# Mask products in couples, and the last rows of two weight matrices stacked, in a two-layer attention and expert kernel

## What is computed

```python
x = L0_attn_x                                  # (8, 512, 256)
xn = layernorm(x)
# layer 0: causal attention, 16 heads of 64, rotary q and k, and a dense gated FFN of 768
sim = q @ k.T * scale
sim = where(causal, sim, -inf)
s = softmax(sim) @ v @ Wo + bo
g = silu((silu(xn @ wg.T) * (xn @ wu.T)) @ wd.T)
x = x + s * g
xn = layernorm(x)
# layer 1: attention without a mask, 16 heads of 16, and 8 experts; expert e takes 64 tokens of each batch
s = attention1(xn)
gate = einsum('becd,edf->becf', xe, w1)        # d = 256, f = 704
up   = einsum('becd,edf->becf', xe, w3)
out  = einsum('becf,efd->becd', silu(gate) * up, w2)
x = x + s * silu(out)
```

## Time and profile before

| what | value |
|---|---|
| median of 3 executions | 2100.8 us (2099.96 to 2102.17) |
| the profiled execution's own time | 2100.51 us |
| its span, first to last instruction | 2098.8 us |
| PE busy | 1930.3 us, 92% |
| DVE, ACT, POOL busy | 1442.2, 1288.3, 666.4 us |
| mean granted TensorE clock | 0.977 |

### The profile page before, as it was taken

How to read it: one execution, slowest core, us unless ns; L and a number is a source line. 1 busy time by engine, 2 the same in 40 slices (tenths; PEclk the granted TensorE clock), 3 DMA queues, 4 the chain that set the end, 5 groups by cost and what they waited for, 6 DMA issues and landing times. The chain is left out here.

```text
span 2098.8 us, 39214 instructions
## 1 busy us (share of the span) xinstructions
PE 1930.3 (92%) x12160; PEld 1474.2 (70%) x12160; DVE 1442.2 (69%) x2908; ACT 1288.3 (61%) x3069; POOL 666.4 (32%) x1032
## 2 busy tenths in 40 slices
PE   1999999999999999999999689994999999999997
PEld 1877878777878788788788578883556556656653
DVE  5785885876858858858678554422777777777773
ACT  3675674664656746646566565531686786776774
POOL 0353452543543534525435223332001011011012
PEclk9999999999999999999999889997899999999999
DMA  6110211111111111111111373312000011011001
GB/s 221 41 41 25 49 41 33 40 32 42 42 32 41 42 32 44 39 42 36 26 41 41 118 275 105 103 61 100 4 18 22 30 50 50 0 50 50 0 31 40
DMA packets 72942, 111.82 MB, mean 53 GB/s; under 512 B 5952, under 2 KB 46784, under 8 KB 72256
## 3 DMA queue, kind: packets, MB, share of 16 engines
q1 hardware_dynamic: 72224, 108.62, 17.5%
q10 hardware_dynamic: 544, 1.05, 0.2%
HBM read 55.12 MB, written 20.97 MB: 36 GB/s over the span
## 5 line engine op out<-in xcount | busy, mean ns | idle before, releaser
L1518 DVE TENSOR_REDUCE nm<-ps 128x1 f32<-128x512 f32 x512 | 336.8, 687 | 114.6 <-PE ps L1377 110.8
L1629 ACT ACTIVATE pt<-pst 128x512 f32<-128x512 f32 x512 | 296.0, 602 | 142.4 <-PE pst L1385 141.4
L805 POOL TENSOR_SCALAR pr<-pr,rinv 128x128 f32<-128x128 f32 (+3 forms) x512 | 264.8, 538 | 359.4 <-DVE rinv L691 359.4
L570 ACT ACTIVATE pr<-sc,nmax 128x128 f32<-128x128 f32 (+3 forms) x512 | 266.2, 528 | 141.3 <-DVE nmax L680 139.8
L811 POOL TENSOR_TENSOR qk<-ra,rb 128x256 f32<-128x256 f32 x256 | 183.9, 740 | 243.5 <-DVE rb L702 187.6
L680 DVE TENSOR_REDUCE nmax<-sc 128x1 f32<-128x128 f32 (+3 forms) x512 | 219.9, 483 | 57.8 <-PE sc L405 57.6
L1377 PE MATMUL ps<-kb,qb 96*128 96x512 f32 x512 | 238.2, 467 | 12.6 <-DVE nm L1518 10.0
L1385 PE MATMUL pst<-qb,kb 128*128 128x512 f32 x512 | 208.1, 408 | 6.7 <-ACT pt L1629 3.6
L403 PE MATMUL sc<-k,qs 128*128 128x256 f32 (+2 forms) x512 | 205.4, 403 | 1.3 <-DMA k<-k 1.2
L1377 PEld LDWEIGHTS ps<-kb,qb 96*128 96x128 f32 x512 | 97.7, 191 | 144.2 <-DVE nm L1518 95.6
L417 PE MATMUL w<-ident,pr 128*128 128x128 f32 x1280 | 172.1, 282 | 22.7 <-DVE rb L702 18.1
(11 more groups left out here) (203 smaller groups left out, 4703.5 us busy)
## 6 DMA issues: line engine op xcount, KB each, us to landing
k<-k SPq DMA_DIRECT2D x256, 128.0 KB, 2.2
raw<-in_w SPq DMA_DIRECT2D x16, 704.0 KB, 5.5
raw<-in_w SPq DMA_DIRECT2D x8, 640.0 KB, 5.1
xa<-in_x SPq DMA_DIRECT2D x2, 2048.0 KB, 13.8
x<-in_x SPq DMA_DIRECT2D x8, 512.0 KB, 3.6
x_scratch<-x SPq DMA_DIRECT2D x8, 512.0 KB, 3.4
xt_hi_scratch<-xt_hi SPq DMA_DIRECT2D x1, 4096.0 KB, 13.6
xt_lo_scratch<-xt_lo SPq DMA_DIRECT2D x1, 4096.0 KB, 23.3
```

What stands on the lines that cost most here:

```text
L570: act.activation(pr[:, h, SOFF[i]:SOFF[i] + (i + 1) * P], sc[:, bank, at:at + (i + 1) * P], ACT.Exp, bias=nmax[:, h, i:i + 1], accum_out=r ...
L805: pool.tensor_scalar(p, p, rinv[:, h, i:i + 1], 1.0, ALU.mult, ALU.mult).then_inc(scaled, 1)
L1518: dve.tensor_reduce(nm[:, g % 2, i, h:h + 1], ps[:, i % 2, :], AXX, ALU.max, negate=True).then_inc(max_done, 1)
L1629: act.activation(pt[:, g % 2, h, i, :], pst[:, i % 2, :], ACT.Exp).then_inc(exp_done, 1)
```

## The change

Two parts. In `scores` the mask product of an even tile is not issued behind its own two products but behind those of the odd tile that follows, directly ahead of that tile's mask product. Tiles 0 and 1, which share a bank, become one group of sums: tile 1's first product no longer starts one, and only the mask product of tile 0 is without the stop flag. `s_done` still goes up by 1 for each mask product.

In `experts` the 64 rest columns of w3 are loaded into the 64 padding columns of w1's tile, so that one group of six products gives gate (partitions 0 to 63) and up (64 to 127) of the rest, and w3's tiles shrink from 768 to 640 columns. Silu writes its 64 rows to partitions 64 to 127, the multiply and the high part stay there, and DVE, in place of POOL, writes the low part to partitions 0 to 63 of the same block of `hh`, behind its split of w2. The rest rows of w2 are loaded twice, to both halves of the partitions, and the block's down products are two for each token tile in place of three. The padding memsets on POOL and the waits for them go.

```diff
@@ layer0, scores
-                        pe.matmul(out, q, k1[:, h, 0:width], start=True, stop=False)
+                        pe.matmul(out, q, k1[:, h, 0:width], start=(i != 1), stop=False)
                         pe.matmul(out, q, k2[:, h, 0:width], start=False, stop=False)
-                        pe.matmul(sc[:, bank, at + i * P:at + (i + 1) * P], c.identb[:], c.maskb[:],
-                                  start=False, stop=True).then_inc(s_done, 1)
+                        for m in (i - 1, i) if i % 2 else ():
+                            bank, at = score(m)
+                            pe.matmul(sc[:, bank, at + m * P:at + (m + 1) * P], c.identb[:], c.maskb[:],
+                                      start=False, stop=(m > 0)).then_inc(s_done, 1)
@@ experts, tiles
+FM1 = (NF1 - 1) * P
-        r1, r3 = (t.sb(f"raw{n}", [P, NC, FP1]) for n in (1, 3))
+        r1, r3 = (t.sb(f"raw{n}", [P, NC, width]) for n, width in ((1, FP1), (3, FM1)))
-        w1h, w1l, w3h, w3l = (t.sb(n, [P, 2, NC, FP1], F32R) for n in ("w1h", "w1l", "w3h", "w3l"))
+        w1h, w1l = (t.sb(n, [P, 2, NC, FP1], F32R) for n in ("w1h", "w1l"))
+        w3h, w3l = (t.sb(n, [P, 2, NC, FM1], F32R) for n in ("w3h", "w3l"))
+        GU1 = 2 * NF1 - 1
+        def rows_of(f):
+            return slice(FR1, P) if f == NF1 - 1 else slice(0, P)
@@ experts, sync
-                    sp.dma_start(r3[:, :, 0:F1], io.w3[one].rearrange("o (c p) f -> p (o c) f", p=P)).then_inc(w13_in, 16)
+                    w3 = io.w3[one].rearrange("o (c p) f -> p (o c) f", p=P)
+                    sp.dma_start(r1[:, :, F1:FP1], w3[:, :, FM1:F1]).then_inc(w13_in, 16)
+                    sp.dma_start(r3[:], w3[:, :, 0:FM1]).then_inc(w13_in, 16)
-                    sp.dma_start(r2[0:FR1, NF1 - 1:NF1, :], io.w2[one, full:F1].rearrange("o p n -> p o n")).then_inc(w2_in, 16)
+                    for h in range(2):
+                        sp.dma_start(r2[h * FR1:(h + 1) * FR1, NF1 - 1:NF1, :], io.w2[one, FM1:F1].rearrange("o p n -> p o n")).then_inc(w2_in, 16)
-                        sp.wait_ge(pad_set, 3)
@@ experts, gpsimd
-                pool.memset(r2[FR1:P, NF1 - 1, :], 0.0).then_inc(pad_set, 1)
-                pool.wait_ge(pad_set, 1)
-                pool.memset(r1[:, :, F1:FP1], 0.0).then_inc(pad_set, 1)
-                pool.memset(r3[:, :, F1:FP1], 0.0).then_inc(pad_set, 1)
-                    for f in range(NF1):
+                    for f in range(NF1 - 1):
@@ experts, scalar: ffn
-                            act.activation(sg[:, f % 2, :], w[:, 2 * f % 4, :], ACT.Silu).then_inc(silu_done, 1)
+                            src = slice(0, FR1) if f == NF1 - 1 else slice(0, P)
+                            act.activation(sg[rows_of(f), f % 2, :], w[src, 2 * f % 4, :], ACT.Silu).then_inc(silu_done, 1)
-                            act.copy(hh[:, f - 1, :], hid[:, (f - 1) % 2, :]).then_inc(hid_hi_done, 1)
+                            part = rows_of(f - 1)
+                            act.copy(hh[part, f - 1, :], hid[part, (f - 1) % 2, :]).then_inc(hid_hi_done, 1)
@@ experts, vector: ffn
-                            dve.wait_ge(hid_lo_done, NF1 * e + f - 1)
-                        dve.tensor_tensor(hid[:, f % 2, :], w[:, (2 * f + 1) % 4, :], sg[:, f % 2, :],
+                            dve.wait_ge(hid_lo_done, (NF1 - 1) * e + f - 1)
+                        part, bank = rows_of(f), (2 * f + (f < NF1 - 1)) % 4
+                        dve.tensor_tensor(hid[part, f % 2, :], w[part, bank, :], sg[part, f % 2, :],
                                           ALU.mult).then_inc(hid_done, 1)
                         if f in (2, 4, 5) and not last:
                             split(e + 1, 1 - u, {2: 0, 4: 1, 5: 2}[f])
+                    f = NF1 - 1
+                    dve.wait_ge(hid_hi_done, NF1 * e + NF1)
+                    dve.tensor_tensor(hh[0:FR1, f, :], hid[FR1:P, f % 2, :], hh[FR1:P, f, :].bitcast(F32),
+                                      ALU.subtract).then_inc(tail_lo_done, 1)
@@ experts, tensor: ffn
-                        for j, (wh, wl) in enumerate(((w1h, w1l), (w3h, w3l))):
+                        for j, (wh, wl) in enumerate(((w1h, w1l), (w3h, w3l))[:1 if f == NF1 - 1 else 2]):
-                    for f in range(NF1):
+                    for f in range(NF1 - 1):
...
+                    f = NF1 - 1
+                    pe.wait_ge(hid_hi_done, NF1 * e + NF1)
+                    pe.wait_ge(tail_lo_done, e + 1)
+                    for i in range(NT):
+                        a = hh[:, f, i * P:(i + 1) * P]
+                        pe.matmul(dn[:, i, 0:C], a, w2h[:, u, f, :], start=False, stop=False)
+                        pe.matmul(dn[:, i, 0:C], a, w2l[:, u, f, :], start=False, stop=True).then_inc(down_done, 1)
```

More of the change, by code:

```diff
@@ L907, in experts @@
         hid_lo_done = t.sem("hid_lo_done1")
+        tail_lo_done = t.sem("tail_lo_done")
         down_done = t.sem("down_done1")
@@ L914, in _ @@
             def _(sp):
-                full = (NF1 - 1) * P
                 def load13(e):
@@ L931, in load2 @@
                         sp.wait_ge(lo2, e)
-                    sp.dma_start(r2[:, 0:NF1 - 1, :], io.w2[one, 0:full].rearrange("o (f p) n -> p (o f) n", p=P)).then_inc(w2_in, 16)
-                    sp.dma_start(r2[0:FR1, NF1 - 1:NF1, :], io.w2[one, full:F1].rearrange("o p n -> p o n")).then_inc(w2_in, 16)
+                    sp.dma_start(r2[:, 0:NF1 - 1, :], io.w2[one, 0:FM1].rearrange("o (f p) n -> p (o f) n", p=P)).then_inc(w2_in, 16)
+                    for h in range(2):
+                        sp.dma_start(r2[h * FR1:(h + 1) * FR1, NF1 - 1:NF1, :], io.w2[one, FM1:F1].rearrange("o p n -> p o n")).then_inc(w2_in, 16)
                 def load(e):
@@ L983, in split @@
                     if part < 2:
-                        act.wait_ge(w13_in, 32 * e + 32)
+                        act.wait_ge(w13_in, 48 * e + 48)
                         act.copy((w1h, w3h)[part][:, u], (r1, r3)[part][:]).then_inc(hi13, 1)
                     else:
-                        act.wait_ge(w2_in, 32 * e + 32)
+                        act.wait_ge(w2_in, 48 * e + 48)
                         act.copy(w2h[:, u], r2[:]).then_inc(hi2, 1)
@@ L992, in ffn @@
                         if f < NF1:
-                            act.wait_ge(gate_up_done, 2 * NF1 * e + 2 * f + 1)
+                            act.wait_ge(gate_up_done, GU1 * e + 2 * f + 1)
                             if f > 1:
                                 act.wait_ge(hid_done, NF1 * e + f - 1)
-                            act.activation(sg[:, f % 2, :], w[:, 2 * f % 4, :], ACT.Silu).then_inc(silu_done, 1)
+                            src = slice(0, FR1) if f == NF1 - 1 else slice(0, P)
+                            act.activation(sg[rows_of(f), f % 2, :], w[src, 2 * f % 4, :], ACT.Silu).then_inc(silu_done, 1)
                         if f > 0:
                             act.wait_ge(hid_done, NF1 * e + f)
-                            act.copy(hh[:, f - 1, :], hid[:, (f - 1) % 2, :]).then_inc(hid_hi_done, 1)
+                            part = rows_of(f - 1)
+                            act.copy(hh[part, f - 1, :], hid[part, (f - 1) % 2, :]).then_inc(hid_hi_done, 1)
                         if f in (1, 3, 5) and not last:
@@ L1028, in _ @@
                     if b == SPLIT:
-                        act.wait_ge(pad_set, 3)
-                        act.wait_ge(w13_in, 32)
+                        act.wait_ge(w13_in, 48)
                         act.copy(w1h[:, 0], r1[:]).then_inc(hi13, 1)
@@ L1033, in _ @@
                 turned_hi(B - 1)
-                act.wait_ge(w2_in, 32)
+                act.wait_ge(w2_in, 48)
                 act.copy(w2h[:, 0], r2[:]).then_inc(hi2, 1)
@@ L1056, in ffn @@
                         dve.wait_ge(silu_done, NF1 * e + f + 1)
-                        dve.wait_ge(gate_up_done, 2 * NF1 * e + 2 * f + 2)
+                        dve.wait_ge(gate_up_done, GU1 * e + min(2 * f + 2, GU1))
                         if f > 1:
-                            dve.wait_ge(hid_lo_done, NF1 * e + f - 1)
-                        dve.tensor_tensor(hid[:, f % 2, :], w[:, (2 * f + 1) % 4, :], sg[:, f % 2, :],
+                            dve.wait_ge(hid_lo_done, (NF1 - 1) * e + f - 1)
+                        part, bank = rows_of(f), (2 * f + (f < NF1 - 1)) % 4
+                        dve.tensor_tensor(hid[part, f % 2, :], w[part, bank, :], sg[part, f % 2, :],
                                           ALU.mult).then_inc(hid_done, 1)
@@ L1130, in ffn @@
                     pe.wait_ge(g_done, NT * e)
-                    for f in range(NF1):
+                    for f in range(NF1 - 1):
                         pe.wait_ge(hid_hi_done, NF1 * e + f + 1)
-                        pe.wait_ge(hid_lo_done, NF1 * e + f + 1)
+                        pe.wait_ge(hid_lo_done, (NF1 - 1) * e + f + 1)
                         for i in range(NT):
@@ L1137, in ffn @@
```

(6 more changed lines are left out.)

1 line of the change is left out of this document (removed).

## The result

The changed kernel takes 2077.32 us (median of four executions, 2075.82 to 2081.08), the kernel before beside it 2101.24 (2099.96 to 2102.17): a ratio of 0.9889, 95% interval 0.9872 to 0.9906. The forecast was 2080.0. The profiled execution took 2076.42 us by its own time, with a span of 2074.7 against 2098.8. Faster was right; some of the terms that make up the sum were not.

What follows compares the result with a forecast made beforehand. The prediction took PE to bound layer 0 and the experts. From the profiled 2100.51 us it took 6.0 for layer 0 and 14.7 for the experts, giving 2079.8, or 2080.0 against the median; range 2070.5 to 2088.5.

Steps and rivals of the forecast that it cites:

- The experts: Per expert, six products of 512 columns and four down products go from PE's path: 1.84 us, 14.7 for eight.
- Rival D: In the experts, the rest's low part comes later than the 2.0 us to spare allow: 2088 us, chance 0.06.
- 0.070 for a mask behind a mask: In the scores, the second mask's price, taken near the lower bound 0.057; a couple saves 0.057 us.
- DVE 0.36 us later: In head 0's scores, tile 2's late mask delays DVE by 0.36 us; pairs 2 to 5 absorb it.
- its two halves gain nothing: In pair 6, PE waits for the low parts, so no couple counts and the pair is 0.36 us longer.
- Pair 0 likewise: In pair 0, savings only lengthen PE's wait; most of the delay is hidden, 0.10 us taken (bounds 0 and 0.36).
- Pair 1 gained 0.11 as forecast: In pair 1, savings before DVE's first copy only lengthen PE's wait; two couples, at 0.057 us each, remain.
- Pair 7 keeps its 4 couples: In pair 7, all four couples count at 0.057 us each; in the last batch 0.18 of delay is taken off.
- Layer 0 as a whole: Layer 0: 0.79 us for each of batches 0 to 6, 0.5 for the last, 6.0 us less together.
- Rival A: In layer 0, delays are hidden everywhere and every couple counts: 2071.2 us in total, chance 0.14.
- Rivals B and C: B: second mask costs a transpose, delays met in full, 2088.4, chance 0.16; C: DVE bounds regular pairs, 2108.8, chance 0.04.
- Before the first expert: Loads ahead of the first expert: the new piece delays w3's, its cast shrinks; 0 taken, bounds 0.25 less and 0.6 more.

Runs made afterwards that it cites:

- late_rest: The changed kernel with two extra DVE row reductions over raw w2 ahead of its split of w2, in seven of eight experts: 2085.98 us, ratio 0.9938.
- masks_doubled: The changed kernel with each mask product issued twice in a row, four masks in a row in place of two: 2097.24 us, ratio 0.9986.
- masks_only: The kernel before with only the masks in couples, experts as before: 2091.35 us, ratio 0.9962.

## Why the prediction was right, and where its terms were off

The forecast was 2080.0 and 2077.32 was measured: the way the change works was right, the experts' term was 0.35 us too large, and layer 0's was 2.9 us too small.

**The experts** were right term by term: 23.14 us forecast and 23.14 measured, Silu 0.2 us behind the group's end, nothing on PE's path. The time to spare was 1.86 for 2.0, and late_rest found 1.75 by delaying the chain. Of 14.7 us 14.35 came out; the last expert's missing 0.36 stands in the wait of attention 1, which the forecast didn't follow. Rival D has no support.

**"0.070 for a mask behind a mask" was mis-sized.** It is 0.057, by 0.28/4 = 0.070 saved per couple, and 0.056 by masks_doubled: its own columns and nothing for its load. I should have followed the reason I gave (behind a mask stands a short load) to its end, the lower bound. That this load is the reason is still not shown: no run put another short product there, with other weights or of another type. For pairs 2 to 5 this is 32 x 0.05 = 1.6 us more. By the 81 ns for 128 columns in the Trainium skill, TensorE: Matmul & The Clock Gate, section Back-to-back issue gap, the couple would have saved 0.046; the trace does not agree with it for two bf16 products of the same weights.

**"DVE 0.36 us later"** was close at its place and too much behind it. DVE comes to tile 2 at 537.58 - 535.76 = 1.82 us behind the scores' begin; before it was 1.48, by the split of its 1.76 us that the prediction made. But the two maxima that follow take 1.16 us where that split left 1.23, and only 0.27 is passed on. That pairs 2 to 5 absorb it was right. Pair 6 was forecast 0.36 longer and is 0.21: +0.28 by the second couple, less 0.07 by the first, which the forecast's "its two halves gain nothing" left out. Pair 0 likewise: +0.03 (+0.10 and -0.07) for a forecast of 0.10. Pair 1 gained 0.11 as forecast, by two couples of 0.057; two at the measured 0.070 would be 0.14.

**"Pair 7 keeps its 4 couples"** was near, but overlooked a wait. It gains 0.16 us for 0.23 forecast, while four couples at the measured 0.070 would give 0.28: the rest is the wait for POOL, whose scaling now ends after PE's masks do. I had checked DVE's list in every kind of pair and POOL's in none. In the last batch pair 7 was forecast 0.18 longer and is 0.25 (10.69 to 10.94 up to the output projection); this falls in the stage that follows layer 0 in the table.

**Layer 0 as a whole.** Where the clock stays up, a batch now gains 4 x 0.28 + 0.11 + 0.16 - 0.03 - 0.21 = 1.15 us. Seven batches give 8.05; the last, with five pairs shorter, pair 6 longer (9.94 to 10.21) and pair 0 by 0.03, 5 x 0.28 - 0.27 - 0.03 = 1.1. That makes 9.15, and less the 0.25 of the last pair 8.9 for 6.0 forecast; masks_only has 8.0 by its ratio (5 to 11 by the interval). Of the 2.9 missing, 1.6 is the price in pairs 2 to 5; pairs 0 and 6 lose less, by some 1.7, and pair 7 gains less, by some 0.5. The profiles' -11.1 holds another 2.0 that is not the change's: pairs 0 and 1 were long in five batches of one execution, by 5.3 us together, and in three of the other, by 3.3. I had looked at pair 0 in batch 3 alone, where it is clean; the forecast never asked whether the eight batches agree.

**The sum.** With the measured prices it is 2100.5 - 8.9 - 14.35 = 2077.2, for 2077.32 measured here and 2074.09 when the same kernel ran again. That it meets the median to 0.1 is luck: between the two profiles the clock alone moved layer 0 by 2.0 us and attention 1 was 1.8 longer. Rival A (every couple counts) was right that the forecast took too little off, but pairs 0 and 6 did lose, and pairs 1 and 7 gained less than their four couples save. Rivals B and C fell with the 0.057 and with the pairs of 12.92.

**Before the first expert** 0 was as good as can be told. The packets under 512 bytes rose from 5952 to 8256, and ACT's wait by 0.13 us, within what the stage varies. By the Trainium skill, DMA: Bandwidth & Descriptors, section Specifications, transfers below 512 bytes don't reach the full rate; no loss from it can be told here.

**Still open:** why the same idle time of PE lets the clock fall in one batch and not in another, at the end of pair 0 and ahead of the dense FFN alike. The transposes show that the idle time has a part at the former place; other ways to fill it were not tried, and nothing was tried at the latter. Open too is why a mask between two tiles' products costs more than its columns.

## What to carry to other kernels

Issue small products of the same kind behind each other: the second cost only its columns here (0.057 us), while one alone between large products cost 0.127. Whether they must share their weights, as the masks do, was not tested. Price such a reordering place by place, because what becomes ready later is absorbed where its reader has slack and paid in full where it has none, and go through every reader's list, the slow engine's too. Where a loop body should take the same time in every round, compare the rounds before pricing it: every difference of over 0.8 us between equal rounds was the clock here, and filling a wait of PE of over 2 us with unused work gave 4 us here, half of what the masks gave.

## What had not been expected of the hardware

- A bf16 product of 128 columns behind another with the same weights starts 0.056 us later; alone in front of another tile's products it had cost 0.127 in the mean.
- Behind PE's idle 2.3 to 2.6 us the granted clock was 0.53 over the next 3.5 us in some batches (17 or 18 matmuls for 28 to 30) and 1.00 in others, with the same instructions. With 16 transposes in the idle time it fell there in none of the eight batches of the one profile, and the kernel was 4 us faster.
- Behind PE's idle 1.7 to 1.9 us ahead of the dense FFN it fell in some batches too, and the FFN behind it then took 1.6 us more.
- The four norm instructions of 0.40 us each made pair 1 0.72 us longer when they stood together; one to a pair they cost PE nothing that its timeline shows (12.92 with and without).
